# Rewriting the qkv and output stages of a four-layer model: three rounded products for one fp32 product

## The reference

```python
xn = layer_norm(x, norm_w, norm_b)
q = (xn @ q_w + q_b).reshape(Bx, Tx, H, -1)
k = (xn @ k_w + k_b).reshape(Bx, Tx, H, -1)
...
v = ((xn @ v_w + v_b) * src_mask[:, :, None]).reshape(Bx, Tx, H, -1)
y = jnp.einsum('bnmh,bmhl->bnhl', att, v).reshape(Bx, Tx, Dx)
e = jax.nn.silu(emb) @ emb_w + emb_b
scale, shift = jnp.split(e[:, None, :], 2, axis=2)
h = layer_norm(y, sb_norm_w, sb_norm_b) * (1.0 + scale) + shift
h = jax.nn.silu(h) @ out_w + out_b
return x + h
```

## Time and profile before

| | us |
|---|---|
| median of the runs | 5598.69 |
| profiled execution, its own time | 5595.86 |
| its span, first to last instruction | 5594.1 |
| TensorE busy | 5031.5 |
| VectorE busy | 4221.7 |
| POOL busy | 3508.2 |
| ScalarE busy | 3206.4 |
| qkv stage, first DMA to the next stage's first VectorE work | 379.1 |
| output stage, first DMA to the next stage's first POOL work | 168.6 |

### The profile page before, as it was taken

How to read it: one execution, slowest core, us unless ns; L and a number is a source line. 1 busy time by engine, 2 the same in 40 slices (tenths; PEclk the granted TensorE clock), 3 DMA queues, 4 the chain that set the end, 5 groups by cost and what they waited for, 6 DMA issues and landing times. The chain is left out here.

```text
span 5594.1 us, 61508 instructions
## 1 busy us (share of the span) xinstructions
PE 5031.5 (90%) x19712; PEld 2643.2 (47%) x19712; DVE 4221.7 (75%) x5622; ACT 3206.4 (57%) x5915; POOL 3508.2 (63%) x2340
## 2 busy tenths in 40 slices
PE   7888989888888878998999999999998888988898
PEld 2333333333333323444444444444443467776777
DVE  6999999999999993227777777777773565656565
ACT  3757575666657552335888888888885124232323
POOL 3879797978888771114898888988887022222222
PEclk9999999999999999997999999999999999999999
DMA  4021212112120204322111111111111211112211
GB/s 174 23 106 38 91 74 78 76 53 80 49 97 33 106 0 168 127 98 46 24 36 35 24 35 24 35 35 24 36 24 50 111 66 70 44 63 71 75 39 68
DMA packets 119633, 350.65 MB, mean 63 GB/s; under 512 B 13104, under 2 KB 14352, under 8 KB 104912
## 3 DMA queue, kind: packets, MB, share of 16 engines
q1 hardware_dynamic: 102448, 300.76, 16.1%
q0 software_dynamic: 9216, 33.56, 1.6%
q10 hardware_dynamic: 7648, 12.41, 0.6%
HBM read 278.49 MB, written 67.67 MB: 62 GB/s over the span
## 5 line engine op out<-in xcount | busy, mean ns | idle before, releaser
L425 POOL TENSOR_TENSOR mamba_hc<-mamba_h,mamba_bc 128x1024 f32<-128x1024 f32 x512 | 1218.0, 2379 | 359.9 <-DVE mamba_h L658 306.1
L805 PE MATMUL mamba_y<-mamba_hc,ident 128*128 128x512 f32 x2048 | 998.4, 611 | 272.4 <-POOL mamba_hc L425 270.7
L1282 POOL TENSOR_TENSOR attn_pair_sum<-attn_pair_sum,attn_prob 128x1024 f32<-128x1024 f32 x512 | 1204.4, 2386 | 53.7 <-ACT attn_prob L1397 53.7
L1441 DVE TENSOR_REDUCE attn_mx<-attn_ps_max 128x1 f32<-128x512 f32 x1536 | 967.6, 685 | 318.0 <-PE attn_ps_max L1305 313.2
L528 ACT ACTIVATE mamba_da<-mamba_dt,mamba_a_neg 128x512 f32<-128x512 f32 x1024 | 691.0, 689 | 718.9 <-DVE mamba_h L658 715.3
L1397 ACT ACTIVATE attn_prob<-attn_ps_s 128x512 f32<-128x512 f32 x2048 | 1051.4, 602 | 76.1 <-PE attn_ps_s L1332 76.1
L658 DVE TENSOR_TENSOR_SCAN mamba_h<-mamba_da,mamba_state,mamba_h 128x512 f32<-128x512 f32 x768 | 941.2, 1269 | 1.9 <-ACT mamba_da L528 1.9
L1332 PE MATMUL attn_ps_s<-attn_q_stack,attn_k_stack 100*128 100x512 f32 x2048 | 885.9, 436 | 5.2 <-ACT attn_prob L1397 5.2
L1305 PE MATMUL attn_ps_max<-attn_k_stack,attn_q_stack 98*128 98x512 f32 x2048 | 834.6, 412 | 33.6 <-DMA attn_q_stack<-qk_parts 16.0
L805 PEld LDWEIGHTS mamba_y<-mamba_hc,ident 128*128 128x128 f32 x2048 | 367.5, 191 | 855.1 <-POOL mamba_hc L425 454.6
L648 DVE TENSOR_TENSOR mamba_h<-mamba_du,mamba_bc 128x1024 f32<-128x1024 f32 x512 | 620.8, 1212 | 65.2 <-POOL mamba_state L427 57.0
(11 more groups left out here) (274 smaller groups left out, 7099.3 us busy)
## 6 DMA issues: line engine op xcount, KB each, us to landing
mamba_bc<-bc_dram SPq DMA_DIRECT2D x64, 1024.0 KB, 7.0
mamba_w<-in_in_proj_w_T SPq DMA_DIRECT2D x16, 2048.0 KB, 7.7
qk_parts<-qkv_pair POOLq DMA_DIRECT2D x64, 512.0 KB, 3.2
attn_k_stack<-qk_parts SPq DMA_DIRECT2D x96, 256.0 KB
attn_q_stack<-qk_parts SPq DMA_DIRECT2D x96, 256.0 KB
mamba_x_in<-in_x SPq DMA_DIRECT2D x16, 1024.0 KB, 5.2
mamba_w<-in_out_proj_w_T SPq DMA_DIRECT2D x8, 2048.0 KB, 8.1
lin_norm_x<-x_after_L SPq DMA_DIRECT2D x16, 1024.0 KB, 5.8
```

Source lines behind the costliest of these rows:

```text
L425: nc.gpsimd.tensor_tensor(hc[:, gs % HC_SLOTS, :, :], h[:, gs % H_SLOTS, :, :], bc[:, g, G:2 * G, :], ALU.mult).then_inc(s["hc_done"], 1)
L805: mm = nc.tensor.matmul(y[ct % 2][:, :], ident[:, :], hc[:, gs % HC_SLOTS, j, :], start=(g == 0 and j == 0), stop=(g == NG - 1 and j == G ...
L1282: nc.gpsimd.tensor_tensor(pair_sum[(hd * NGRP + g) % 2][:, at], first[:, at], prob[unit % SLOTS][:, at], ALU.add).then_inc(s["sum_done"], 1)
L1441: nc.vector.tensor_reduce(to, ps_max[seq % BANKS][:, :], AX.X, ALU.max, negate=own_block(i)).then_inc(s["bank_read"], 1)
```

## The change

In both stages the fp32 operands become rounded pairs. ScalarE cuts the weights to their first part, and POOL or VectorE subtracts to get the second. Of the rows there are two sets of both parts, `xn_first[it % 2]` and `xn_second[it % 2]`, so that the next chunk's can be made while this chunk's are in use. The evacuated rows are made twice from the same banks: rounded by ScalarE (`m.turned`), and in full, back into `m.x` (`full_x`), by VectorE in qkv and by ScalarE in the output stage; POOL's `split_x` subtracts one from the other. Each fp32 product becomes three rounded ones (`PARTS`).

In qkv the transposes of the next chunk move from the chunk's end to behind its sixth q/k group (`TURN_AT` = 5). `full` and `vb` are gone: v is biased straight into its place, ScalarE rounds a q/k bank straight into the pair, and VectorE makes the second half from the bank, which TensorE may fill again when that is done (`second_done`). In the output stage TensorE does first-part products of tiles 0 and 1, then their last parts, then the next chunk's transposes, then tiles 2 and 3; VectorE norms the next chunk ahead of this chunk's additions.

The films are split in two pieces each, rows and fold, and stand between chunks: film 1 in qkv at chunks 4 and 5, films 2 and 3 in the output stage behind chunks 3 and 4, and 5 and 6. They use the transposes' banks. SP loads the qkv film only when all three weights have landed, and the next rows only when POOL's parts of the chunk before are made.

```diff
@@ stage_qkv, TensorE
             def chunk(it, c, more):
-                pe.wait_ge(w_in[2], 16)
+                rows_t = (xn_first[it % 2], xn_second[it % 2])
+                pe.wait_ge(w_split[2], 1)
                 for t in range(TT):
                     pe.wait_ge(s["v_biased"], it * TT + t - 1) if t >= 2 else pe.wait_ge(s["v_biased"], it * TT)
                     for k in range(KD):
-                        if t == 0:
-                            pe.wait_ge(m.turned, it * KD + k + 1)
-                        mm = nc.tensor.matmul(bank[t % 2][:, :], m.xn_t[:, k, t * P:(t + 1) * P], w[2][:, k, :],
-                                              start=(k == 0), stop=(k == KD - 1))
+                        for i, j in PARTS:
+                            if t == 0:
+                                pe.wait_ge(s["second_x"] if i else m.turned, it * KD + k + 1)
+                            mm = nc.tensor.matmul(bank[t % 2][:, :], rows_t[i][:, k, t * P:(t + 1) * P], (w_first, w_second)[j][2][:, k, :],
+                                                  start=(k == 0 and i + j == 0), stop=(k == KD - 1 and i == 1))
                     mm.then_inc(s["v_mm"], 1)
+                if it == FILM_ROWS:
+                    pe.wait_ge(s["full_x"], (it + 1) * KD)
+                    film_rows_pe(nc, pe, film)
...
                 for i in range(NQ):
...
-                    pe.wait_ge(s["full_done"], it * NQ + i - 1) if i >= 2 else pe.wait_ge(s["full_done"], it * NQ)
+                    pe.wait_ge(s["second_done"], it * NQ + i - 1) if i >= 2 else pe.wait_ge(s["second_done"], it * NQ)
...
-                if it + 1 < NCH:
-                    norm_pe(nc, pe, m, it + 1)
+                    if i == TURN_AT and it + 1 < NCH:
+                        pe.wait_ge(s["full_x"], (it + 1) * KD)
...
+                        norm_pe(nc, pe, m, it + 1)
@@ stage_qkv, VectorE
                 for i in range(NQ):
                     dve.wait_ge(s["first_done"], it * NQ + i + 1)
-                    nc.vector.tensor_tensor(pair[:, i % 2, 1, :], full[:, i % 2, :], pair[:, i % 2, 0, :].bitcast(F32),
-                                            ALU.subtract).then_inc(s["second_done"], 1)
+                    which, mt = divmod(i, KD)
+                    nc.vector.scalar_tensor_tensor(out=pair[:, i % 2, 1, :], in0=bank[2 + i % 2][:, :], scalar=qk_bias[which][:, mt:mt + 1],
+                                                   in1=pair[:, i % 2, 0, :].bitcast(F32), op0=ALU.add, op1=ALU.subtract
+                                                   ).then_inc(s["second_done"], 1)
+                    if i == TURN_AT and it + 1 < NCH:
+                        full_x(it + 1)
                     if i == NORM_AT and it + 1 < NCH:
                         norm(it + 1)
@@ POOL, both stages
+def split_x(nc, pool, m, first, second, full_made, second_made, it):
+    for k in range(KD):
+        pool.wait_ge(m.turned, it * KD + k + 1)
+        pool.wait_ge(full_made, it * KD + k + 1)
+        nc.gpsimd.tensor_tensor(by_tile(second[:, k, :]), in_x(m, k), by_tile(first[:, k, :].bitcast(F32)),
+                                ALU.subtract).then_inc(second_made, 1)
+PARTS = ((0, 0), (0, 1), (1, 0))
@@ stage_out, TensorE
+            for it in range(NCH):
+                for t in range(2):
+                    if it:
+                        pe.wait_ge(s["out_done"], it * TT - TT + t + 1)
+                    products(it, t, PARTS[:2], True, False)
+                for t in range(2):
+                    products(it, t, PARTS[2:], False, True).then_inc(s["o_mm"], 1)
                 if it + 1 < NCH:
+                    pe.wait_ge(s["full_x"], (it + 1) * KD)
...
                     norm_pe(nc, pe, m, it + 1)
+                for t in range(2, TT):
+                    if it:
+                        pe.wait_ge(s["out_done"], it * TT - TT + t + 1)
+                    products(it, t, PARTS, True, True).then_inc(s["o_mm"], 1)
+                for f, rows_at, fold_at in zip(films, ROWS_AT, FOLD_AT):
+                    if it == rows_at:
+                        pe.wait_ge(s["full_x"], (it + 2) * KD)
+                        film_rows_pe(nc, pe, f)
...
@@ stage_out, VectorE
+            for it in range(NCH):
+                if it + 1 < NCH:
+                    norm(it + 1)
+                for t in range(TT):
+                    dve.wait_ge(s["o_mm"], it * TT + t + 1)
...
```

More of the change, by code:

```diff
@@ L161, in film_pe, with film_rows_dve, film_fold_dve @@
     mm.then_inc(f.made, 1)
-def film_dve(nc, dve, f):
+def film_rows_dve(nc, dve, f):
+    for half in range(2):
+        dve.wait_ge(f.row_made, half + 1)
+        nc.vector.tensor_copy(f.row[:, half * D:(half + 1) * D], f.ps_row[half][:, :]).then_inc(f.row_copied, 1)
+def film_fold_dve(nc, dve, f):
     _, bias, norm_w, norm_b = FILMS[f.layer]
@@ L167, in film_dve @@
     on_batches = lambda v: v.unsqueeze(2).to_broadcast([P, KD, NB])
-    for half in range(2):
-        dve.wait_ge(f.row_made, half + 1)
-        nc.vector.tensor_copy(f.row[:, half * D:(half + 1) * D], f.ps_row[half][:, :]).then_inc(f.row_copied, 1)
     dve.wait_ge(f.made, 1)
@@ L972, in stage_qkv @@
         w_in = [r.sem(f"w_in_{n}") for n in "qkv"]
-        names = "small_in mask_done mask_stored v_mm v_biased v_done qk_mm full_done first_done second_done own_dve"
+        w_cut = [r.sem(f"w_cut_{n}") for n in "qkv"]
+        w_split = [r.sem(f"w_split_{n}") for n in "qkv"]
+        names = "small_in mask_done mask_stored v_mm v_biased v_done qk_mm first_done second_done full_x second_x own_dve"
         s = {n: r.sem(n) for n in names.split()}
@@ L981, in stage_qkv @@
         NORM_AT = 1
-        films = [Film(r, keep, i + 1, spare[:, i * (QT // 2):(i + 1) * (QT // 2), :],
-                      [bank[0], bank[1], bank[2 + i]]) for i in range(2)]
+        TURN_AT = NQ - 3
+        FILM_ROWS, FILM_FOLD = NC_B, NC_B + 1
+        film = Film(r, keep, 1, spare[:, :, :], m.bank)
         @block.sync
@@ L989, in chunk @@
                 if it + 1 < NCH:
+                    sp.wait_ge(s["second_x"], (it + 1) * KD)
                     norm_load(sp, m, src, it + 1)
             norm_load(sp, m, src, 0)
-            sp.wait_ge(m.x_loaded, 16)
-            for film in films:
-                film_load(sp, film, a)
+            for i in range(3):
+                sp.wait_ge(w_in[i], 16)
+            film_load(sp, film, a)
             for b in range(NB):
@@ L1092, in norm, with full_x @@
                 dve.wait_ge(m.x_loaded, (it + 1) * 16)
-                norm_dve(nc, dve, m, own, it, lambda t: m.x[:, t, :])
+                norm_dve(nc, dve, m, own, it, lambda t: m.x[:, t, :], (s["second_x"], it * KD))
                 own.end()
+            def full_x(it):
+                for k in range(KD):
+                    dve.wait_ge(m.turned, it * KD + k + 1)
+                    nc.vector.tensor_scalar(in_x(m, k), by_tile(m.bank[k][:, :]), g[:, k:k + 1], bvec[:, k:k + 1],
+                                            ALU.mult, ALU.add).then_inc(s["full_x"], 1)
             norm(0)
-            for film in films:
-                film_widen(nc, dve, film)
+            dve.wait_ge(w_cut[2], 1)
+            nc.vector.tensor_tensor(w_second[2][:, :, :], w_raw[2], w_first[2][:, :, :].bitcast(F32), ALU.subtract).then_inc(w_split[2], 1)
+            full_x(0)
+            film_widen(nc, dve, film)
             dve.wait_ge(s["small_in"], 48)
@@ L1118, in _ @@
                 each_chunk(dve, b, lambda it: None, chunk)
-            for film in films:
-                film_dve(nc, dve, film)
 def stage_attention(nc, a, keep, parts, mask_parts, v):
@@ L1543, in _ @@
         def _(pool):
+            norm_pool(nc, pool, m, 0)
             for it in range(NCH):
[L1545 removed]
+                split_x(nc, pool, m, xn_first[it % 2], xn_second[it % 2], s["full_x"], s["second_x"], it)
+                if it + 1 < NCH:
+                    norm_pool(nc, pool, m, it + 1)
         @block.tensor
         def _(pe):
[L1549 to L1561 removed]
@@ L1563, in _, with products @@
-            for b in range(NB):
-                each_chunk(pe, b, lambda it: norm_pe(nc, pe, m, it) if it == 0 else None, chunk)
-            pe.wait_ge(s["out_done"], NCH * TT)
-            film_pe(nc, pe, film_3)
+            def products(it, t, parts, first, last):
+                rows_t = (xn_first[it % 2], xn_second[it % 2])
+                for k in range(KD):
+                    for i, j in parts:
+                        if t == 0:
+                            pe.wait_ge(s["second_x"] if i else m.turned, it * KD + k + 1)
+                        mm = nc.tensor.matmul(bank[t][:, :], rows_t[i][:, k, t * P:(t + 1) * P], (w_first, w_second)[j][:, k, :],
+                                              start=first and k == 0 and (i, j) == parts[0],
+                                              stop=last and k == KD - 1 and (i, j) == parts[-1])
+                return mm
```

218 lines of the change are left out of this document (131 added, 87 removed).

## The result

The changed kernel takes 5543.88 us (median of four runs, 5539.89 to 5547.37), the kernel before, measured beside it, 5598.79 (5592.84 to 5600.03): a ratio of 0.9905, 95% interval 0.9889 to 0.9921, 54.9 us less. The forecast was 5545.

The account below looks back on a forecast made before the run. TensorE's products bound qkv; VectorE's norm and the residual's load share the out stage's bound. Savings of 33.7 (qkv), 19.3 (out) and 0.7 (before chunk 1) make 53.7: 5542.2 us profiled, 5545 at the median, range 5528 to 5568.

Parts of the forecast that it names:

- Products: Both stages: three rounded products of 0.2335 us replace one fp32 product, 0.700 for 0.858; a qkv chunk 33.6 for 41.2.
- Rival C: A rounded product takes 0.2145 us instead of 0.2335, giving 5523 us; chance 0.04.
- The wait in qkv: Ahead of the fifth q/k group TensorE waits 2.86 us for VectorE's second part, queued behind the norm, in seven chunks.
- The clock behind it: TensorE's clock falls after each of the seven qkv waits, costing 1.6 us each.
- A: The clock doesn't fall in the qkv waits: 7 x 1.6 less, 5534 us; chance 0.25.
- B: Half clock loses 2.9 us per qkv wait, and the out stage's waits 1.6 each: 5566 us; chance 0.17.
- First chunk: In qkv the first tile's products wait for POOL's parts and TensorE starts at half clock: 2 to 5 us, 3.5 taken.
- Films: One film between qkv's chunks costs 5.5 us; the out stage's two cost 7 to 11, 9.2 taken.
- Sum for qkv: The qkv stage from its first product takes 327.8 us for 361.5, 33.7 less.
- Output stage: Chunks 15.0 us apart, TensorE waiting 2.06 (drawn 1.9) for VectorE's norm without clock loss; 116.8 for 136.1 from chunk 1.
- D: In qkv a pair's store lands in 5.8 us for 3.2, costing 0.85 a group, 54 us: 5599; chance 0.04.
- E: TensorE stays at half clock after its 14 waits, 14 us each, 90 lost: 5624 us; chance 0.05.

Follow-up runs that it names:

- norm_split: Changed kernel with qkv's next-chunk norm cut in two, statistics behind the fourth v tile, normalization behind the second q/k pair: 5521.57 us, 0.9868.
- mask_bank: Changed kernel with VectorE scaling the mask row into a free PSUM bank instead of SBUF, so its subtraction reads PSUM: 5545.34 us, 0.9907.

## Why the prediction was right, and where its steps were not

The total, 53.7 less, met the profiled 56.0 and the medians' 54.9. Its parts did so less well.

**Products.** 0.2335 us was right: additions to v stand 2.80 apart for 12 products, and q's and k's products start 0.229 to 0.233 apart. Rival C is out.

**The wait in qkv.** Drawn 2.71 was forecast, 2.80 to 2.90 came, in seven chunks of seven, released by VectorE's second part. The chain behind it was the forecast one too, as norm_split shows: take the norm from ahead of the third pair, and the wait goes. A chunk without a fall is 38.18; the working gives 33.6 + 1.75 + 2.86 = 38.2.

**The clock behind it.** This step failed in part: 1.6 was the right price and seven the wrong count. In the kernel before, 1.62 is what the second stretch of 2.52 cost: from 5575.84 to 5579.33 eight products took 3.49 us, at a granted clock of 0.51, for 1.87 at 0.2335 each. Behind the first the next products started 0.30 and 0.23 apart, at a clock of 1.00. A fall in each of the seven chunks, as the sum has it, no run shows. There were three falls in the first profile (4.9 us instead of 11.2), five in the second. Over the six profiles that have such waits unfilled it was 24 of 37. So A and B were each true of some chunks; the row of 2.52 that fell once and once not the earlier trace rows already said that an average was due, not one value for all.

**First chunk.** This step failed. 3.5 was forecast, 10.4 came (21.6 less 11.2). The mechanism named, TensorE waiting for POOL's parts and starting at half clock, is worth 2.4 (13.6 less 11.2, in mask_bank). Most of that are the waits: the granted clock was 0.50 over the transposes ahead (2146.0 to 2150.5, first profile) and 0.84 from 2150.52 to 2152, and in mask_bank 1.00 from 2152.6 on. The other 8 are VectorE's mask row, which the prediction didn't list: work that nobody had edited, but that the change had put beside POOL's new subtraction of weights, with v's additions queued behind it.

**Films.** 3.56 for the rows and 1.70 for the fold in qkv, 5.3 for 5.5. In the output stage the four pieces are 10.5, and the waits beside three of them shrank by 1.8 (1.26, 1.69 and 1.26 instead of 2.00): 8.7 for 9.2.

**Sum for qkv.** 328.2 for 327.8: the first chunk's 6.9 too little and the clock's 6.3 too much cancel.

**Output stage.** The wait is 2.00 for the 1.9 forecast and a chunk 15.16 for 15.0. The step "1.9 idle, less than the 2.52 that once kept the rate, so no loss" failed: the clock fell behind all three waits of 2.00 in both profiles, 3 x 1.6 = 4.8 us. The length of the idle stretch alone does not order the falls: in the four profiles that have them, the clock fell behind eleven of twelve such waits of 2.00, behind 24 of 37 of 2.80 to 2.90 in qkv, and behind none of the twelve of 1.26 to 1.70 in the later chunks. In the output stage's first chunk, where TensorE had just stopped several times for POOL's parts, it fell behind waits of 1.34 to 1.53 in four of five profiles, and behind the four of 2.02 to 2.05 in qkv's first chunk each time. The trace of the kernel before already held a row against the step, which the earlier trace rows does not show: in the linear stage a stretch of 2.08, soon after one of 14.5, was followed by eight slow products, beside stretches of 2.13, 2.44 and 2.44 that were not.

```profile
4496.24 0.50 PE L1777 MATMUL lin_mm_bank<-lin_xn_first,lin_w_k_first 128*128 128x512 f32 x1 [2.08 <-POOL lin_w_k_second L1732]
...
4497.27 0.63 PE L1777 MATMUL lin_mm_bank<-lin_xn_first,lin_w_k_first 128*128 128x512 f32 x1
```

The last chunk was 15.9 (4408.29 to 4424.23) for 17.6 forecast, mostly since a tile's store lands in 2.0 us, not 3.2, and the part ahead of chunk 1 gained 3.1 instead of 0.7. Together 18.4 for 20.0.

**Rivals D and E.** The pairs' store lands in 3.2 as before, and there is no wait ahead of every group. The mean clock is 0.97 in qkv and 0.96 in the output stage, no slow stretch behind a wait is longer than some 5 us, half of what E needed.

**Slips in the working.** The norm's first statistic follows 0.08 us less than the duration before it (0.69 less 0.61), not 0.06; L+1.83 is worked out with 0.08. B's terms add up to 5565, not 5566. Neither matters.

That the forecast came within two us of the median is partly luck: two errors of over six us cancelled in qkv, 4.3 came from outside the two stages in the profiled run, and the second measurement of the same kernel gave 46.8 for the forecast 53.7.

## What to carry to other kernels

When a change lets an engine read a bank that another one used to copy, the bank's release moves into that engine's queue: look at what stands ahead of it there (here six us of norm) and cut or move that first; it was worth more (26 us of 328) than any other edit. List the unedited work of each engine beside which the change puts something new, small instructions too, and above all VectorE work with two SBUF operands beside POOL (here 4.5 to 9.0 us for 0.28). A wait of two or three us can cost more than its length: here slow products followed most of them and cost 1.6 us each time, so count these as well.
